# A two-layer cross-attention, quantised FFN and MoE kernel: wider payload rows, paired first norms, tanh for silu, and router work between the expert tiles

## What is computed

```python
x = x + tanh(g_xattn[0]) * L0_xattn(ctx, layernorm(x), W_b)
x = x + tanh(g_ffn[0]) * L0_ffn(layernorm(x), ...)
x = x + tanh(g_xattn[1]) * L1_xattn(layernorm(x), ctx, ctx, mask, ...)
x = x + tanh(g_ffn[1]) * L1_ffn(layernorm(x), wqkv, w1, w2)
```

## Time and profile before

| | |
|---|---|
| runs shown | 394.52, 395.03, 395.2 us; median 395.03 |
| profiled execution | 393.35 us, span 391.6 us |
| mean granted clock of TensorE | 0.844 |
| busy PE / DVE / ACT / POOL | 274.4 (70%) / 197.5 (50%) / 128.2 (33%) / 117.9 (30%) us |
| DMA | 37.11 MB in 34797 packets, of which 8990 under 512 B and 26901 under 2 KB |

### The profile page before, as it was taken

How to read it: one execution, slowest core, us unless ns; L and a number is a source line. 1 busy time by engine, 2 the same in 40 slices (tenths; PEclk the granted TensorE clock), 3 DMA queues, 4 the chain that set the end, 5 groups by cost and what they waited for, 6 DMA issues and landing times.

```text
span 391.6 us, 6241 instructions
## 1 busy us (share of the span) xinstructions
PE 274.4 (70%) x2067; PEld 187.9 (48%) x2067; DVE 197.5 (50%) x681; ACT 128.2 (33%) x288; POOL 117.9 (30%) x262
## 2 busy tenths in 40 slices
PE   6696246657668989878869865683948198999900
PEld 5596231043232334333333423582938198999900
DVE  4768986987741315527742863870364022222214
ACT  4245136461132251242233402321351034544400
POOL 3324840007500000200064160355207543444420
PEclk9699955557997999989978986797798679999965
DMA  7100099816000000000001019216511566874037
GB/s 199 37 0 3 29 333 309 228 9 149 0 3 0 0 2 2 0 2 0 2 15 44 0 57 305 91 40 196 164 50 50 197 192 176 220 210 131 28 107 215
DMA packets 34797, 37.11 MB, mean 95 GB/s; under 512 B 8990, under 2 KB 26901, under 8 KB 34767
## 3 DMA queue, kind: packets, MB, share of 16 engines
q1 hardware_dynamic: 29856, 23.35, 22.1%
q0 software_dynamic: 4160, 12.99, 10.0%
q10 hardware_dynamic: 751, 0.38, 0.4%
HBM read 22.52 MB, written 14.49 MB: 95 GB/s over the span
## 4 chain that ended last, share of the span: by engine, by line
PE 43%; DVE 25%; issue 10%; ACT 7%; POOL 4%; DMA 4%; another core or an unknown queue 3%; SPq 1%; POOLq 0%; DVEq 0%; ACTq 0%
PE wide L1007 12%; PE bank L1016 4%; PE duo L1016 3%; DVE mC L1257 2%; DVE h L1143 2%; DVE amh L1244 2%; DMA space<-expert_out 2%; DVE space L1240 2%; PE bank L901 2%; PE wide L880 2%; ACT space L572 2%; PE bank L904 2%; PE wide L884 2%; DMA wd<-in_w_down 1%
## 5 line engine op out<-in xcount | busy, mean ns | idle before, releaser
L1007 PE MATMUL wide<-space,w1r 128*128 128x128 f32 x468 | 63.2, 288 | 0.0
L1433 DVE TENSOR_TENSOR space<-space,wide 128x384 f32<-128x384 f32 x39 | 21.6, 554 | 76.1 <-PE wide L1007 38.8
L1007 PEld LDWEIGHTS wide<-space,w1r 128*128 128x128 f32 x468 | 59.6, 204 | 0.0
L445 POOL DMA_INDIRECT expert_out<-space x39 | 38.5, 988 | 46.4 <-ACT space L646 43.0
L387 POOL TENSOR_SCALAR rvp<-mv 128x4 f32<-128x4 f32 (+1 forms) x11 | 2.6, 235 | 157.3 <-DVE mv L1078 157.0
L434 POOL DMA_INDIRECT expert_rows<-pay,slot x32 | 31.2, 976 | 39.0 <-DVE slot L1367 25.2
L1016 PE MATMUL bank<-w_s,space 128*128 x120 | 18.8, 296 | 17.0 <-DVE space L1433 11.2
L1257 DVE TENSOR_REDUCE mC<-wide 128x8 f32<-128x616 f32 x22 | 16.9, 792 | 22.3 <-PE duo L860 14.6
L572 ACT ACTIVATE space<-wide 103x512 f32<-103x512 f32 (+1 forms) x32 | 17.1, 602 | 32.5 <-PE wide L884 20.1
L639 ACT ACTIVATE space<-wide 128x384 f32<-128x384 f32 x39 | 19.2, 492 | 19.8 <-remote 8.6
L1016 PEld LDWEIGHTS bank<-w_s,space 128*128 128x128 f32 x120 | 16.2, 205 | 18.3 <-issue 18.3
(11 more groups left out here) (253 smaller groups left out, 564.5 us busy)
## 6 DMA issues: line engine op xcount, KB each, us to landing
w1r<-in_w1T SPq DMA_DIRECT2D x39, 352.0 KB
expert_rows<-blank POOLq DMA_DIRECT2D x2, 2970.0 KB, 17.9
expert_rows<-blank POOLq DMA_DIRECT2D x1, 2574.0 KB, 28.5
space<-expert_rows SPq DMA_DIRECT2D x39, 66.0 KB
space<-expert_out SPq DMA_DIRECT2D x8, 256.0 KB, 3.2
xs<-in_x SPq DMA_DIRECT2D x4, 256.0 KB, 5.2
w_s<-in_w2T SPq DMA_DIRECT2D x2, 512.0 KB, 5.2
out<-xs SPq DMA_DIRECT2D x4, 256.0 KB, 3.5
```

The costliest lines, as they stand in the source:

```text
L445: pool.indirect_dma_start(planes, bass.IndirectOffsetOnAxis(ap=mpay[:, i % XRING, D:D + 1].bitcast(I32), axis=0), my[:, i % XRING, :], Non ...
L1007: ins = pe.matmul(wide[:, 2 * (i % 2) + g, c * P:(c + 1) * P], w1r[:, i % RING, g * F + F0[c]:g * F + F0[c] + P], mhT[:, i % 2, :])
L1433: dve.tensor_tensor(mhidT[:, i % 2], msil[:, i % 2], wide[:, 2 * (i % 2) + 1, 0:NF * P].rearrange("p (c t) -> p c t", c=NF), ALU.mult).the ...
```

## The change

1. ROW goes from D + 4 to D + 16 words, so a payload row has 576 bytes and not 528. Token (p j) and not (j p) lies in partition p, for x, out, expert_out, the mask and the token numbers: a partition's share of a batch is one piece of 2 KB.
2. DVE makes all four first reciprocal roots, two batches at a time (`pair_stats`, `pair_sums`, `rsqrt` with `over`): the statistics of batches 2 and 3 stand between the steps of the first, the norms of batches 0 and 1 between the steps of the second. The norm of batch 2 before stage B (`late_norm`) stands between the steps of batch 3's. The orders of stage A on DVE, PE and ACT are new, and `weights_B` and `weights_B2` come later. PE's first two `keep_warm` go from 24 to 36 products.
3. POOL waits for the first unit of stage B before it makes `pick`, clears the table and sets its constants.
4. In the loop of stage B the maxima are taken over two chunks and one chunk (`hid_max`), 8 instructions for 12, with two of three multiplications directly behind each other.
5. The value products of the last batch go through one half of the heads and then the other; ACT does the first half's reciprocal ahead of router(2) step 0.
6. In the expert tiles ACT makes tanh(gate / 2) and DVE one more instruction, (tanh + 1) * gate; the weight of a token is multiplied by 0.5. ACT's order of tables is set once by hand, before router(2) step 1. The blocks that load, `e_silu` and `e_tanh`, are otherwise alike.
7. DVE's router step 1 has three parts, and the parts stand behind e_mul 0 (batch 2) and 4, 5, 6 (batch 3), step 2 behind 1 and 7. On PE the routers stand inside a tile, ahead of its down product; the weight offsets are loaded behind the phase's first transpositions. POOL's order is two scatters, send(2), two scatters, send(3), the rest.

```diff
-    ROW = D + 4
+    ROW = D + 16
...
-    SENT = 6
+    SENT = (2, 4)
...
-x_v = x.rearrange("b (j p) d -> b p j d", p=P)
...
+x_v = x.rearrange("b (p j) d -> b p j d", p=P)
...
-    for n in rsqrt_turns[0:NB]:
+    for n in rsqrt_turns[0:NB - 1]:
         rsqrt(n)
...
+    pool.wait_ge(gu_psum, 1)
...
     rsqrt(rsqrt_turns[-1])
+    for i in range(SENT[0]):
+        scatter(i)
     send(2)
-    for i in range(SENT):
+    for i in range(SENT[0], SENT[1]):
         scatter(i)
     send(3)
-    for i in range(SENT, NTILE):
+    for i in range(SENT[1], NTILE):
         scatter(i)
...
         expT(b, 2, 1)
-        if b >= 1:
+        if 1 <= b < NB - 1:
             router(b - 1, 0)
     recip(NB - 1, 0)
+    router(NB - 2, 0)
     recip(NB - 1, 1)
+    act.add_instruction(mybir.InstLoadActFuncSet(name=nc.get_next_instruction_name(), act_func_set_id=0, ins=[], outs=[],
+                                                 engine=mybir.EngineType.Activation))
     router(NB - 2, 1)
...
-        act.activation(msil[:, i % 2], wide[:, 2 * (i % 2), 0:NF * P].rearrange("p (c t) -> p c t", c=NF),
-                       ACT.Silu).then_inc(e_sil, 1)
+        act.activation(mth[:, i % 2], wide[:, 2 * (i % 2), 0:NF * P].rearrange("p (c t) -> p c t", c=NF),
+                       ACT.Tanh, scale=0.5).then_inc(e_sil, 1)
...
         if i + 1 < end:
-            e_silu(i + 1)
+            e_tanh(i + 1)
...
-    router(NB - 2, 2)
-    e_silu(f)
...
-        if i == 3:
+        if i == 2:
             router(NB - 1, 0)
...
+        if i == 4:
+            router(NB - 1, 1)
+        if i == 5:
+            router(NB - 1, 2)
+    for f, e in PHASES:
+        first(f)
+        e_tanh(f)
+        if f == 0:
+            router(NB - 2, 2)
+        for i in range(f, e):
+            tile(i, e)
...
     A0(0)
-    A1(0)
     A0(1)
-    A2(0)
+    A1(0)
     A1(1)
     A0(2)
+    A2(0)
+    A1(2)
     A3(0)
     A0(3)
-    A1(2)
-    A1(3)
     A2(1)
+    A1(3)
     A3(1)
...
-    for t in range(TR):
-        for half in range(2):
+    for half in range(2):
+        for t in range(TR):
             pv(b, half, t)
...
             e_up(i + 1)
-        e_down(i, w)
...
-        if i == 0:
+        if i == 1:
             router(b - 1, 2)
...
+        if i == 7:
+            router(b, 2)
+        e_down(i, w)
+    pe.wait_ge(ld_exp, 16 * NF)
+    pe.wait_ge(lap_zero, 1)
+    for k, (f, e) in enumerate(PHASES):
+        pe.wait_ge(turns_ready, k + 1)
+        first(f)
+        for i in range(f, e):
+            if (i - f) % RING == 0:
+                w = places(i, min(RING, e - i))
+            tile(i, e, w[(i - f) % RING])
...
-        return n == 0 or n == 2 * NB - 1 or n == 4 * NB - 2
+        return n < NB or n == 2 * NB - 1 or n == 4 * NB - 2
...
             ins.then_inc(dve_chain, 1)
-            n, j = divmod(at[0], TB)
-            at[0] += 1
-            if n < NB:
-                if j == 0:
-                    dve.wait_ge(ld_x[n], 16)
-                bn_stat(n, j)
+            if over:
+                over(step[0])
+            step[0] += 1
             dve.wait_ge(dve_chain, n_chain[0])
...
-        normalise(NB + b, h[:, b % 2])
+        if b != NB - 2:
+            normalise(NB + b, h[:, b % 2])
         link(dve.tensor_reduce(amx[:, b:b + 1], h[:, b % 2], AX.XY, ALU.max, apply_absolute_value=True))
...
-    first_stats()
-    normalise(0, h[:, 0])
-    weights_B()
-    A1(0)
-    normalise(1, h[:, 1])
+    def next_stats(k):
+        if k < 2 * TB:
+            n, j = 2 + k // TB, k % TB
+            if j == 0:
+                dve.wait_ge(ld_x[n], 16)
+            bn_stat(n, j)
+    def first_norms(k):
+        if k < 2 * TB:
+            ins = normal(k // TB, k % TB, h[:, k // TB])
+            if k % TB == TB - 1:
+                ins.then_inc(h_ready, 1)
+    def late_norm(k):
+        n = 2 * NB - 2
+        if k == 0:
+            dve.wait_ge(rstd_ready, rsqrt_turns.index(n) + 1)
+            dve.wait_ge(hT_psum, n - 1)
+        if k < TB:
+            ins = normal(n, k, h[:, n % 2])
+            if k == TB - 1:
+                ins.then_inc(h_ready, 1)
+    pair_stats(0)
+    pair_sums(0)
+    rsqrt(mv[:, 0:2, :, 1], rstd[:, 0:2, :], rv[:, 0:2], rt[:, 0:2], next_stats)
+    pair_sums(2)
+    rsqrt(mv[:, 2:4, :, 1], rstd[:, 2:4, :], rv[:, 2:4], rt[:, 2:4], first_norms)
     normalise(2, h[:, 0])
-    A2(0)
+    A1(0)
     normalise(3, h[:, 1])
     A1(1)
-    A3(0)
+    weights_B()
     A1(2)
+    A2(0)
+    A3(0)
     A1(3)
-    weights_B2()
     A2(1)
     A3(1)
+    weights_B2()
     A2(2)
...
     A4(1)
-    A3(3)
+    A3(3, late_norm)
...
+    def hid_max(b, c, z):
+        n = FC[z - 1][1]
+        dve.wait_ge(hid_ready, NF * b + z)
+        return dve.tensor_reduce(amh[0:n, b, c:z], hid[0:n, b, c:z, :], AX.X, ALU.max, apply_absolute_value=True)
     for u in range(NB * NF):
...
                                  op0=ALU.mult, op1=ALU.mult).then_inc(hid_ready, 1)
-        dve.wait_ge(hid_ready, u + 1)
-        ins = dve.tensor_reduce(amh[0:n, b, c:c + 1], hid[0:n, b, c, :], AX.X, ALU.max, apply_absolute_value=True)
-    link(ins)
+        if c == 2:
+            hid_max(b, 0, 2)
+        if c == 0 and b >= 1:
+            hid_max(b - 1, 2, 3)
+    link(hid_max(NB - 1, 2, 3))
...
-            link(dve.tensor_scalar(gr[:], gr[:], th[:, 3:4], None, ALU.mult))
+            link(dve.tensor_scalar(gr[:], gr[:], th[:, 3:4], 0.5, ALU.mult, ALU.mult))
...
     def e_mul(i):
         if i >= 2:
...
         dve.wait_ge(e_sil, i + 1)
+        link(dve.scalar_tensor_tensor(out=msil[:, i % 2], in0=mth[:, i % 2], scalar=1.0,
+                                      in1=wide[:, 2 * (i % 2), 0:NF * P].rearrange("p (c t) -> p c t", c=NF),
+                                      op0=ALU.add, op1=ALU.mult))
         dve.wait_ge(e_w1, i + 1)
...
         if i == 0:
-            router(b - 1, 2)
+            router(b - 1, 1, 2)
         if i == 1:
+            router(b - 1, 2)
             plan(1)
...
             router(b, 0)
-        if i == 6:
+        if i == 4:
             router(b, 1, 0)
-        if i == PHASES[0][1] - 1:
+        if i == 5:
             router(b, 1, 1)
+        if i == 6:
+            router(b, 1, 2)
+        if i == 7:
             router(b, 2)
...
```

146 lines of the change are left out of this document (52 added, 94 removed).

## The result

The changed kernel takes 393.58 us (median of 20 runs, 388.82 to 399.62), the kernel before 394.99 us (20 runs, 392.01 to 399.21). The ratio is 0.9936, 95% interval 0.9911 to 0.9962: faster by 0.6%, some 2.5 us. The ratio and its interval leave out the executions in a slower state that both kernels fall into; the medians over all 20 are 1.4 us apart. I had forecast 387.5 us, 7.5 us less, with a range of 376 to 395. The direction is right, the size is a third. The profiled execution took 392.13 us, span 390.4, against 393.35 and 391.6.

The account below looks back on a forecast made before the run. Bounds: DVE in stage A and stage B's loop, PE in later tiles, waits between. Terms -2.2 + 0.7 - 1.3 - 3.5 - 1.6 + 0.4 = -7.5 us take 395.03 to 387.5 us, range 376 to 395.

Parts of the forecast that it names:

- Stage A: Stage A: POOL's work moved away and the late norm save time, batch 0's wait and later quantising cost some; -2.2 us.
- POOL's work beside stage B: Stage B: POOL's moved work slows nothing there and gives back 0 us, though up to 4.7 us was possible.
- Loop: Loop of stage B: wider maxima save 0.6 us, waits for banks cost up to 2.0; middle taken, +0.7 us.
- End of C: End of stage C: the first half's three division steps lie beside the second half's products; -1.3 us.
- Tiles: Expert tiles: table loads, DVE's doubled multiplication, router pieces, phase change and bunching together give -3.5 us, bounds -8 and +3.
- The unexplained stretches: Expert tiles: waits without visible cause, 17.5 us of the chain, stay as long as they are.
- Tanh: Expert tiles: three table loads go, -3.8 us; DVE's doubled multiplication costs +3.0 us in tiles 0 to 2, 8 and 9.
- The pieces: Routing between tiles 8 and 9 moves beside tiles 4 to 8: -5.8 us, with +1.3 us as those become DVE's.
- The bunching ahead of tile 2: Expert tiles: the pieces of router(2) with plan(1) bunch ahead of tile 2; +1.0 us.
- Tail: Kernel's end: larger DMA packets shorten the additions' loads, -1.6 us; the last tile's extra DVE step costs +0.4 us.
- The shrinking stretches: Rival, expert tiles: unexplained waits shrink with shorter indirect DMA series or row size, 5 to 12 us more gone; chance 0.2.
- The slower rival: Rival: DVE bounds tiles 1 to 8, second DMA series grows by four or five, tile 9 late; 398 us, chance 0.12.

Follow-up runs that it names:

- p_early: The changed kernel without POOL's wait for stage B, so pick, table clearing and constants come in stage A as before: 397.78 us, ratio 1.0044 to the kernel before.
- sent_old: The changed kernel with POOL's old order, send(2), six scatters, send(3), the rest: 387.93 us, ratio 0.9813 to the kernel before.
- s_paced: The changed kernel with two memsets of a blank tile behind each of POOL's 32 sends: 384.65 us, ratio 0.9728 to the kernel before.
- x_mix: The changed kernel with scatters put between the pairs of DMAs of send(2) and send(3), no memsets: 381.12 us, ratio 0.9658 to the kernel before.
- t_silu: The changed kernel with silu on ACT and one multiplication on DVE, as before: 389.70 us, ratio 0.9871 to the kernel before.
- r_old: The changed kernel with the routers' blocks of batches 2 and 3 back between the tiles on DVE, ACT and PE: 398.13 us, ratio 1.007 to the kernel before.

## Why the prediction was right or wrong

**Stage A (-2.2):** right in the trace, -2.05, by the steps named: the slowing beside POOL gone, which p_early puts at 4.3 us, against 4.7 in the sum, less what the later quantising costs. What I didn't see was the clock: the same stage ends 3 us earlier in executions that keep it up.

**POOL's work beside stage B (0):** right. The multiplications take 739 ns on the mean and the single maxima 671, no more than before, with the clearing and the memsets beside them; `pick` ends at 60.72 and meets only the first multiplication. The rule of the Trainium skill ("SBUF — State Buffer", Who interferes with whom) that I had weighed holds here: the tensor_scalar of the root's step and of the norms is slowed in p_early, the maximum at 51.58 us is not. Stage B's first multiplication comes 0.5 us later behind stage A than before. That is not POOL, which rests until 57.85: PE turns the last h at 52.46, and what it waited for is ACT's late copy.

**Loop (+0.7):** the mechanism was right, the term mis-sized: +1.8. I had computed +2.0 for a batch that waits, and then took the middle between it and a lower bound for a loop that doesn't wait, although the working had just shown that it waits in every batch.

**End of C (-1.3):** right. In the changed kernel the first half's three divisions begin at 236.28, beside the second half's products. From the first division behind them to the residual it is 3.7 us (241.62 to 245.30) and was 4.9 (241.56 to 246.49). The -1.4 of the table agrees, but by itself it lies within what this stage varies by.

**Tiles (-3.5):** this is the term that failed, +0.5, in three places. (1) "The unexplained stretches I leave as long as they are": I gave the new order of POOL's queue no price. sent_old, with that one line undone, is 4.8 us faster, more than the whole 4.0 us that the term missed; s_paced and x_mix show that the pace and the order of POOL's indirect DMAs move the time by 8 and 11 us. In the traces the waits without a cause are 2.2 us longer than before and 6.2 longer than in sent_old. (2) Tanh: I counted -3.8 for three loads "all where a tile waits for ACT" and +3.0 for DVE, 0.8 us to the good; undoing it gave 2.6 us. I had hidden the second instruction everywhere but in five tiles, and t_silu shows it costing from the end of C to tile 4 and behind tile 9, while three of the seven loads that come back lie beside DVE's router. The sum took each part against the old schedule and not against the other parts of the change. (3) The pieces: I had -5.8, of which tiles 4 to 8 give back 1.3. The hole gave 5.0, and these tiles gave back 2.9; by r_old the pieces bring tile 9 no earlier. They are worth 5.3 us all the same, behind tile 9, by a way that I had not seen. The bunching ahead of tile 2, +1.0 in the sum, is +2.3 in the trace (tile 1 to 2 takes 6.0 us and not 3.8).

In the PE-bound tiles I had priced DVE's second instruction at nothing. From tile 17 to 38 it cost 0.8 us, at the places where PE loads offsets.

**Tail (-1.6, and +0.4 for the last tile's step):** mis-sized. From tile 38 to the end it is 20.45 us before and 19.95 in the changed kernel, but 19.9 to 20.7 in the twelve experiments, which have the same tail: a gain isn't shown. Queue 1 has 4800 packets (before 6336):

```profile
q1 hardware_dynamic: 4800, 3.15, 50.8%
```

1536 fewer is what the four stores save. The loads of `expert_out` have kept their pieces of 512 bytes, since the buffer in SBUF holds both planes of a token side by side; that could be read in the code.

**Table loads:** the Trainium skill ("ScalarE: Activation LUTs", What ACT_TABLE_LOAD costs) gives a drain of some 1380 ns on top; by it seven loads more would take up to 7 x 2.66 = 18.6 us, an estimate. In t_silu a load of 1.28 us at 249.60 is followed by its activation at 250.90, 0.02 us behind its end. The rows of this kernel show no drain, and the time went the other way.

**The rivals:** the shrinking stretches (0.2) were the right place to look, in the wrong direction; the waits grew by 2.2 us. The slower rival (0.12) had a second series longer by four or five DMAs; it has 13, as before. Its sign, tile 9's product later than 294 us, did come: the product is at 295.03, with the multiplication at 293.59 where I had forecast some 288. And scatters do bunch up behind send(3): sent_old, where two fewer wait there, is faster.

## What to carry to other kernels

A wait that the profile can't name is not a constant: find out what it goes with (here, indirect DMAs on POOL one behind the other) and price every reordering of that queue first. An order that mixes two kinds of DMAs can be worth more than all the arithmetic between them; here it was 11 us. And a part of a change is to be costed against the schedule that the other parts leave, not the old one: here three of seven table loads would have gone under another wait, and the instruction that replaced them came on the path.

A share or a row called issue is not yet a wait without a cause. Look at the rows of the other engines in the same stretch first: 5.5 us of it here was DVE at work ahead of the product that ACT waited for.

## What the runs showed of the hardware

- While POOL issues indirect DMAs one each 1.27 us, other engines' waits end late: 9.4 us in one case and 10.1 in r_old, with the products that they wait for done. Series of 10 to 15 do it, with rows of 528, 576 or 512 bytes; one each 2.1 us, as in the later tiles, does not, and in x_mix, with at most eight in a row, no wait without a cause in the chain of the tiles is over 1.7 us. Memsets between them, or scatters that wait for their tile, remove most of it. What is late, the product, its semaphore or something else, stays open.
- The granted clock of TensorE in 13 to 20 us of the same code is 0.50 to 0.58 in some executions, 1.00 in others and 0.76 or 0.85 in three; stage A ended at 52.2 us in one of the first kind and at 49.2 in one of the second.
- A DVE maximum over 1024 columns takes 1.20 us, two over 512 take 1.37.
